# Attention: the value products' stationary operand with 32 instead of 17 columns per column group

## What is computed

```python
Q = (query @ Wq.T).reshape(B, QL, HEADS, HEAD_DIM)
K = kv_k.reshape(KV, HEADS, HEAD_DIM)
V = kv_v.reshape(KV, HEADS, HEAD_DIM)
scores = jnp.einsum('bqhd,khd->bhqk', Q, K) * SCALE
attn = jax.nn.softmax(scores, axis=-1)
out = jnp.einsum('bhqk,khd->bqhd', attn, V).reshape(B, QL, HIDDEN)
return out @ Wo.T
```

## Time and profile before

| what | value |
|---|---|
| median of 3 runs | 2264.12 us |
| lowest and highest | 2259.59 and 2273.28 us |
| the profiled execution | 2266.55 us |
| its span, first to last instruction | 2264.8 us |
| granted TensorE clock, mean over the span | 0.931 |
| busy: PE, DVE, ACT, POOL | 2026.0, 1572.4, 1360.1, 261.8 us |

### The profile page before, as it was taken

How to read it: one execution, slowest core, us unless ns; L and a number is a source line. 1 busy time by engine, 2 the same in 40 slices (tenths; PEclk the granted TensorE clock), 3 DMA queues, 4 the chain that set the end, 5 groups by cost and what they waited for, 6 DMA issues and landing times. The chain is left out here.

```text
span 2264.8 us, 40076 instructions
## 1 busy us (share of the span) xinstructions
PE 2026.0 (89%) x15956; PEld 1067.1 (47%) x15956; DVE 1572.4 (69%) x1951; ACT 1360.1 (60%) x2700; POOL 261.8 (12%) x274
## 2 busy tenths in 40 slices
PE   6793999991578999999999999999999999999884
PEld 3552889991223343343343334334334333536663
DVE  3337112215598999998999999999999998215334
ACT  1220444440116888887888888888888888653221
POOL 0001334431020000000000000000000000002462
PEclk9795999995567999999999999999999999979997
DMA  4201668755716000006000005000020000001124
GB/s 138 88 4 65 213 224 258 257 179 139 102 44 69 13 2 13 13 1 69 13 2 13 13 13 57 13 13 1 13 79 2 2 2 2 20 21 25 58 82 153
DMA packets 150034, 140.93 MB, mean 62 GB/s; under 512 B 75506, under 2 KB 122590, under 8 KB 149086
## 3 DMA queue, kind: packets, MB, share of 16 engines
q1 hardware_dynamic: 140446, 112.72, 21.1%
q0 software_dynamic: 9408, 25.70, 3.6%
HBM read 106.40 MB, written 31.72 MB: 61 GB/s over the span
## 5 line engine op out<-in xcount | busy, mean ns | idle before, releaser
L1003 DVE TENSOR_REDUCE maxp<-banks 128x2 f32<-128x1024 f32 x1024 | 1238.8, 1224 | 68.2 <-PE banks L997 61.9
L1435 ACT ACTIVATE pring<-banks 128x512 f32<-128x512 f32 x2048 | 1109.2, 595 | 244.3 <-PE banks L1316 168.2
L1330 PE MATMUL banks<-pring,vcur 128*17 128x256 f32 x8192 | 650.5, 390 | 9.4 <-ACT osb L1429 7.3
L997 PE MATMUL banks<-kst,qst 48*128 48x512 f32 x2048 | 527.5, 513 | 38.4 <-DVE maxp L1003 26.1
L1316 PE MATMUL banks<-qst,kst 50*128 50x512 f32 x2048 | 432.0, 410 | 0.0
L997 PEld LDWEIGHTS banks<-kst,qst 48*128 48x128 f32 x2048 | 196.0, 188 | 474.2 <-issue 344.6
L1330 PEld LDWEIGHTS banks<-pring,vcur 128*17 128x17 f32 x8192 | 136.9, 95 | 325.9 <-issue 182.5
L1316 PEld LDWEIGHTS banks<-qst,kst 50*128 50x128 f32 x2048 | 264.9, 187 | 35.0 <-issue 17.7
L766 ACT ACTIVATE hT<-banks,b 128x128 f32<-128x128 f32 x295 | 108.2, 368 | 186.7 <-PE banks L703 171.1
L904 DVE TENSOR_SCALAR yo<-banks,wblock 128x256 f32<-128x256 f32 x59 | 28.5, 483 | 223.8 <-PE banks L712 223.8
L1301 POOL TENSOR_TENSOR acc<-xn,orec 128x256 f32<-128x256 f32 x15 | 9.3, 621 | 1259.9 <-DVE orec L1480 1259.9
(11 more groups left out here) (304 smaller groups left out, 1312.6 us busy)
## 6 DMA issues: line engine op xcount, KB each, us to landing
w1r<-in_L_ffn_w SPq DMA_DIRECT2D x59, 640.0 KB
kst<-key_parts SPq DMA_DIRECT2D x24, 512.0 KB, 17.7
key_parts<-ksp SPq DMA_DIRECT2D x32, 256.0 KB
w2all<-in_L_ffn_w SPq DMA_DIRECT2D x12, 640.0 KB, 7.7
w2all<-expert_rows SPq DMA_DIRECT2D x12, 512.0 KB, 8.2
qst<-query_parts SPq DMA_DIRECT2D x96, 64.0 KB, 2.3
normed_rows<-xn SPq DMA_DIRECT2D x8, 512.0 KB, 2.9
kf<-in_kT SPq DMA_DIRECT2D x16, 256.0 KB
```

Of the source, the lines that this page charges most:

```text
L997: mm = nc.tensor.matmul(ps[:, base + r, :], qst[i][rows, hp, qt * P:(qt + 1) * P], keys[rows, hp, kb * 512:(kb + 1) * 512], start=True, st ...
L1003: return nc.vector.tensor_reduce(maxp[:, B % 2, :, hp, qt, kb], ps[:, base:base + 2, :], X, ALU.max)
L1330: mm = nc.tensor.matmul(ps[32 * j:32 * j + VC, 7, cols], vcur[g % 2][:, kt, j, :], pring[:, (G % 2) * HG + j, cols], start=(kt == 0 and ha ...
L1435: nc.scalar.activation(pring[:, n % (2 * HG), :], ps[:, n % 3, :], ACT.Exp, scale=float(DH) ** -0.5).then_inc(exp_done, 1)
```

## The change

The two value buffers are made flat and 15 columns longer (`GC - VC`), and the old four-dimensional view is taken of them, so that loads and the column of ones stand where they stood. The value product takes 32 columns from the place where the head's 17 begin: its own 17 and the first 15 of what lies next, which is the next head or the next tile. It writes 32 partitions of bank 7. Rows 17 to 31 of each group then hold products that nobody reads. For the last head of the last tile the 15 columns behind the end are set to zero by POOL, once for each buffer. The tiles that are allocated behind the value buffers begin 128 bytes later. On every engine the order of the instructions is as before, but for the two memsets.

```diff
-            vcur = [sb(f"vcur{i}", [P, NKT, HG, VC], F32, l1) for i in range(2)]
-            aT = vcur[NG % 2][:].rearrange("p t h c -> p (t h c)")[:, 0:KD * S].rearrange("p (k s) -> p k s", k=KD)
+            GC = 32
+            vflat = [sb(f"vcur{i}", [P, NKT * HG * VC + GC - VC], F32, l1) for i in range(2)]
+            vcur = [v[:, 0:NKT * HG * VC].rearrange("p (t h c) -> p t h c", t=NKT, h=HG) for v in vflat]
+            aT = vflat[NG % 2][:, 0:KD * S].rearrange("p (k s) -> p k s", k=KD)
@@
                         for i in range(2):
                             nc.gpsimd.memset(vcur[i][:, :, :, DH], 1.0)
+                            nc.gpsimd.memset(vflat[i][:, NKT * HG * VC:], 0.0)
                         nc.gpsimd.memset(f32(kst[1][:]), 1.0)
@@
                         for j in range(HG):
-                            mm = nc.tensor.matmul(ps[32 * j:32 * j + VC, 7, cols], vcur[g % 2][:, kt, j, :],
+                            c = (kt * HG + j) * VC
+                            mm = nc.tensor.matmul(ps[GC * j:GC * (j + 1), 7, cols], vflat[g % 2][:, c:c + GC],
                                                   pring[:, (G % 2) * HG + j, cols], start=(kt == 0 and half == 0),
                                                   stop=(kt == NKT - 1 and half == 1), skip_group_check=True)
```

## The result

| what | before | after |
|---|---|---|
| median, 20 runs each | 2265.24 us | 2270.86 us |
| lowest and highest | 2259.59, 2273.84 | 2265.56, 2290.73 |
| profiled execution, its span | 2266.55, 2264.8 | 2269.52, 2267.8 |

The medians differ by 5.6 us, a ratio of 1.0025. The recorded ratio is 1.004 with a 95% interval of 1.0022 to 1.0058, nearer to that of the means, 1.0038 (8.7 us). The kernel is slower, by less than 1%, and clear of noise. The forecast was 2271.2 us and +7.1.

The account below looks back on a forecast made before the run. Bound: the loop of second-half scores, two exponentials, first-half value products and maximum product, 2.46 us a tile. Adding 6.3 + 0.8 = 7.1 us to the 2264.1 us median of three runs gave 2271.2 us, range 2257 to 2286.

Parts of the forecast that it names:

- (e): Changes of batch and last batch: second half pays too where nothing covers it, (45 + 20) x 12.4 ns = 0.8 us.
- (a): Weight load of the value products (L1330): fifteen more columns cost 12.4 ns, read from load durations.
- (b): Value groups on PE: only the first load of each group is felt, growing by 12.2 ns; later loads are hidden.
- steep slope from L736: Value weight loads: 1.4 ns a column, 21 ns for fifteen, 21.5 us in all; chance 0.16 together with both halves paying.
- (c): Value loads: the four column groups load beside each other, so 12.4 ns is paid once for four, not four times.
- queueing rival: L1330's loads queue at 32 columns: 2355 us if all eight are felt, 2305 if only the first pass; chance 0.09.
- (d): Steady tile: first half, on the loop, pays 12.4 ns; second, with 20 ns to spare, nothing; 512 tiles make 6.3 us.
- counted over both halves: Value products of both tile halves pay, 1024 x 12.4 ns = 12.7 us, 2276.8 us; chance 0.16 together with a steeper slope.
- (f): Two POOL memsets hidden by DVE's work; 128-byte shift and extra output rows of bank 7 taken to cost nothing.
- DVE as a floor: DVE's reductions, 2.448 us a tile, stop any gain at 0.016 us a tile, 8 us in all: 2256 us.
- rival that it would be faster: An effect outside the value groups makes the kernel faster by over 1%; chance 0.03.

Follow-up runs that it names:

- first32: Changed kernel with 32 columns only in the value products of a tile's first half, 17 in the second; ratio 1.0029 to the kernel before.
- second32: Changed kernel with 32 columns only in the value products of a tile's second half, 17 in the first; ratio 1.0033 to the kernel before.
- layout17: Changed kernel's longer buffers, 128-byte shift and memsets, but value products of 17 columns as before; ratio 1.0005 to the kernel before.
- again32: The changed kernel run once more, unaltered; ratio 1.0038 to the kernel before, median 2247.89 against 2242.37 us.
- cols24: Changed kernel with 24 columns in every value product; ratio 1.0055 to the kernel before.
- cols28: Changed kernel with 28 columns in every value product; ratio 1.0026 to the kernel before.
- cols8: Changed kernel with 8 columns in every value product, leaving out half the features and the sums; ratio 0.9990 to the kernel before.
- cols1: Changed kernel with 1 column in every value product, leaving out all features but the first; ratio 0.9977 to the kernel before.
- swap17: Kernel before (17 columns) with the second maximum unit put ahead of the first half's value products; ratio 1.0109 to the kernel before.
- swap32: Changed kernel (32 columns) with the second maximum unit put ahead of the first half's value products; ratio 1.0162 to the kernel before.

## Why the prediction came out

The forecast came out by its mechanism: each step of it was measured apart, and those that carry the sum held. Two things are less than they look. That the median of 2270.86 us lies 0.3 us from the forecast of 2271.2 is luck: the median of three runs that it was counted from was 1.1 us below that of 20, and the growth was forecast 1.5 us above that of the medians (and 1.6 us below that of the means). And one term, (e), was put too high.

- **The size of the exposed load, (a) and (b).** Put at 12.4 ns for 15 columns; measured 391 to 403 in the first pass, 379 unchanged in the second. The two ways of reading it (the load's own duration, and the first product of a chain against the following ones) agreed beforehand and agreed with the result. The steep slope from L736, 21 ns, was wrong: 1, 8, 17, 24, 28 and 32 columns give 377, 383, 391, 397, 400 and 403 ns, 0.8 a column.
- **Four groups at once, (c).** The load time is paid once for four groups at 32 columns as at 17, so the queueing rival is excluded. The Trainium skill ("TensorE: Matmul & The Clock Gate", Part 3, The mechanism) says that a load overlaps running products only when the row group differs; the same section also names a background weight buffer as another way in. The trace disagrees with the first: the second pass's loads, on all 128 rows, cost nothing from 8 to 32 columns (379 ns). No run here shows what lets them in. The figure of the same page (LDWEIGHTS, loading the stationary operand), one column in 1/1.2 ns, agrees with the step of 0.8 ns a column; a load's whole duration in the rows, 108 ns for 32 columns, is some 80 ns more than the estimate of 27 ns by it.
- **Only the first half pays, (d).** Shown by first32 and second32. This is what halves the cost: counted over both halves it would have been 12.7 us. The 0.02 us of slack, read from rows with two decimals, were 18 ns by the starts, enough for 12; 7 ns are left. (The 1.08 us that the prediction calls two pieces of 1.08 are both exponentials together, and its sum counts them so.)
- **The change of batch, (e).** Put at 12.4 ns for some 65 tiles, 0.8 us. A batch grew by 0.40 us, which is 32 times 12.4 ns, the first half alone; with three tiles paying twice it would be 0.43. The 25 steady tiles carry 0.32 us of it and the other seven 0.08, 11 ns each. first32 and the changed kernel, 81.88 and 81.90 us a batch, differ by 0.02 us. So the part of the term for the changes of batch, 45 tiles or 0.6 us, was put too high: by these rows half of it is there at most. For the twenty tiles of the last batch no run shows anything: from the last POOL row to the last value product it takes 93.1 us before and 95.3 after, but 95.0 with one column, under another clock each time.
- **No cost of layout and memsets, (f).** Shown by the tiles and the recorded ratio of layout17, and by its medians only at equal clock.
- **DVE as a floor.** Not settled; it mattered for none of the sum, only for the rival that it would be faster.
- **The sum.** 16 x 0.40 = 6.4 us by the tiles, 5.6 and 5.5 us in the medians of two comparisons, 7.1 forecast; without (e) the forecast was 6.3. What the steps did not hold is the spread of the runs: 2291 us is 5 us above the range's upper end, though the median is in its middle.

## What to carry to other kernels

In this kernel the weight load of the value products is felt once for each run of eight, at its head, and by its columns; behind that it hides. A few nanoseconds on an engine that is busy 90% of the time need not cost anything: find the loop that closes, by looking for the two places where the idle time ends on another engine, and ask whether the step lies in the loop or beside it. When a wait of 20 ns in a steady loop is traded for another order, look first at the places where the pattern breaks, since one bad change of batch outweighs 25 good tiles. And a cost of 0.3% is read from rows that repeat many times in one trace: here the medians of layout17, which has none of it, rose by 0.2%.

## What was not expected of the hardware

In the first comparison the changed kernel spreads more than the one before, and the clock goes with it. Its mean granted clock was 0.928 or less in 7 of 20 executions. In the repetition, again32, it was so in 2 of 12 against 1 of 23, and the spread was no wider than that of before (2243.8 to 2258.9 against 2224.7 to 2248.9 us). On the chip of layout17, first32, second32 and cols24 it was second32 in 3 of 10, cols24 in 3 of 6 and first32 in 2 of 10, against layout17 in none of 10 and the kernel before in none of 27. It was cols28 in 3 of 12 beside again32, and on the third chip cols8, whose tiles are *shorter*, in 3 of 10, cols1 in none of 8, and swap17 and swap32 in 1 of 4 each, against none of 17 of the kernel before there. So it follows neither from longer tiles nor from more columns.

One place where the clock falls can be seen in the profiled executions. At the change to another head group, near 1,270 us, PE waits for the maxima:

```profile
1272.60 0.61 PE L999 MATMUL banks<-kst,qst 48*128 48x512 f32 x2 [1.53 <-DMA qst<-mrow]
```
```profile
1272.41 0.50 PE L999 MATMUL banks<-kst,qst 48*128 48x512 f32 x2 [2.00 <-DMA qst<-mrow]
```

The first row is second32, where the clock fell behind it, the second layout17, where it stayed at full rate although PE had stood idle for longer. All ten profiled executions with the order of before, by their traces:

| kernel | PE's wait, us | granted clock 0.50, from and to, us | this batch, us | mean clock of the execution |
|---|---|---|---|---|
| before | 1.86 | not here | 83.2 | 0.931 |
| after | 1.70 | not here | 83.5 | 0.931 |
| layout17 | 2.00 | not here | 83.4 | 0.931 |
| first32 | 1.62 | not here | 83.4 | 0.932 |
| second32 | 1.53 | 1272.8 to 1296.7 | 89.0 | 0.927 |
| cols24 | 1.98 | 1279.5 to 1282.9 | 84.4 | 0.929 |
| cols28 | 1.66 | 1270.9 to 1284.6 | 88.2 | 0.930 |
| again32 | 1.55 | 1275.4 to 1285.6 | 86.9 | 0.931 |
| cols8 | 1.78 | 1271.1 to 1281.3 | 86.3 | 0.928 |
| cols1 | 1.59 | 1269.5 to 1279.8 | 86.0 | 0.930 |

In six of the ten the clock was 0.50 for 3 to 24 us at or behind this wait, and the batch took 1 to 6 us more. The waits of the six, 1.53 to 1.98 us, and of the four, 1.62 to 2.00, cover the same lengths, so the length alone does not decide it. Nor does the mean clock of an execution tell of this stretch: four of the six have 0.929 to 0.931, so the counts above are counts of something wider. I suppose that the moment at which the wait falls matters, which any change of the tile time shifts; that is a guess, and no run here tests it.
